# Softmax denominators in six rows of 128 columns, and a 3x3 convolution on two column halves

## What is computed

```
s = jnp.einsum('bhqd,bhkd->bhqk', q, k) / np.float32(np.sqrt(HD))
return jnp.einsum('bhqk,bhkd->bhqd', jax.nn.softmax(s, -1), v)
```

```
x = x + _L1_conv_ref(_gn(x), L1_conv_weight)
t = _to_tokens(x)
```

## Time and profile before

| | |
|---|---|
| median of three runs | 984.92 us (984.06 to 989.01) |
| span of the profiled execution | 980.1 us |
| PE busy | 875.3 us, 89% |
| DVE busy | 595.7 us, 61% |
| ACT busy | 457.1 us, 47% |
| POOL busy | 204.5 us, 21% |
| reciprocals L1676 | 32 of 1756 ns |
| denominators L955 | 1536 instructions, 58.8 us of busy time |
| 3x3 convolution L679 | 80 instructions, 389 ns mean |

### The profile page before, as it was taken

The page is one execution under the profiler, slowest core; times in us unless marked ns, Lnnn a source line. Parts: engine busy times, 40 slices in busy tenths (PEclk is TensorE's granted clock), DMA queues, the critical chain, the costliest instruction groups (busy, mean ns, idle before and its releaser), DMA issues.

```text
span 980.1 us, 22296 instructions
## 1 busy us (share of the span) xinstructions
PE 875.3 (89%) x9216; PEld 588.9 (60%) x9216; DVE 595.7 (61%) x1666; ACT 457.1 (47%) x764; POOL 204.5 (21%) x274
## 2 busy tenths in 40 slices
PE   9888798999999999999999999999988879978876
PEld 8675475566666665666566566656555555644553
DVE  5545534673688468845884588558844764653456
ACT  1003326453555355525543655356435645524754
POOL 1002100120225012401341124112411231131122
PEclk9999689999999999999999999999979999998988
DMA  7100000000000000000000001000100100030000
GB/s 198 25 7 1 1 6 23 23 23 28 23 23 23 28 23 23 23 28 23 23 23 28 7 23 39 23 1 23 39 11 26 36 23 23 23 81 23 2 1 22
DMA packets 25572, 25.84 MB, mean 26 GB/s; under 512 B 14688, under 2 KB 20576, under 8 KB 25344
## 3 DMA queue, kind: packets, MB, share of 16 engines
q1 hardware_dynamic: 25472, 24.42, 8.7%
HBM read 19.69 MB, written 4.72 MB: 25 GB/s over the span
## 4 chain that ended last, share of the span: by engine, by line
PE 58%; DVE 17%; ACT 11%; issue 6%; DMA 5%; POOL 2%; SPq 1%; POOLq 0%; DVEq 0%; ACTq 0%
PE ring L934 7%; PE pv L955 5%; PE side_a L633 5%; PE ring L889 5%; PE pv L973 4%; ACT pr L1190 4%; DVE rden L1676 3%; DMA scale<-branch_scale 3%; PE heads L879 2%; PE side_a L642 2%; PE heads L914 2%; PE ring L929 2%; DMA branch_scale<-rden 2%; PE heads L861 2%; PE ring L897 2%
## 5 line engine op out<-in xcount | busy, mean ns | idle before, releaser
L1190 ACT ACTIVATE pr<-ring 128x1024 f32<-128x1024 f32 (+1 forms) x128 | 120.9, 944 | 108.3 <-PE ring L938 61.0
L934 PE MATMUL ring<-kq 64*128 64x256 f32 (+2 forms) x1280 | 136.5, 341 | 0.7 <-ACT kq L1242 0.5
L934 PEld LDWEIGHTS ring<-kq 64*128 64x128 f32 x1280 | 96.3, 191 | 42.6 <-issue 30.8
L1234 ACT ACTIVATE kq<-ring 128x896 f32<-128x896 f32 x64 | 58.8, 919 | 85.3 <-PE ring L889 85.3
L1686 DVE SCALAR_TENSOR_TENSOR ob<-pv,all_gates,scale 128x256 f32<-128x256 f32 x96 | 46.3, 482 | 85.3 <-PE pv L973 38.4
L1661 DVE TENSOR_REDUCE toks<-heads 128x2 f32<-128x512 f32 x64 | 44.3, 692 | 84.8 <-PE heads L919 83.4
L573 POOL TENSOR_TENSOR toks<-ta,tb 128x128 f32<-128x128 f32 (+1 forms) x96 | 39.7, 434 | 180.4 <-DVE tb L1652 180.4
L1242 ACT ACTIVATE kq<-ring 128x256 f32<-128x256 f32 x64 | 24.6, 384 | 107.5 <-PE ring L897 107.0
L1676 DVE RECIPROCAL rden<-pv 128x256 f32<-128x256 f32 x32 | 56.2, 1756 | 25.5 <-PE pv L955 25.0
L536 POOL TENSOR_TENSOR oT<-ob 128x256 f32<-128x256 f32 x32 | 23.3, 727 | 226.3 <-DVE ob L1686 226.3
L889 PE MATMUL ring<-early,toks 128*128 128x128 f32 x448 | 63.5, 284 | 7.5 <-ACT pr L1190 7.4
(11 more groups left out here) (377 smaller groups left out, 1704.4 us busy)
## 6 DMA issues: line engine op xcount, KB each, us to landing
scale<-branch_scale SPq DMA_DIRECT2D x128, 96.0 KB, 2.3
branch_scale<-rden SPq DMA_DIRECT2D x32, 128.0 KB, 1.7
late<-in_late SPq DMA_DIRECT2D x1, 2158.5 KB, 8.4
xin<-in_x SPq DMA_DIRECT2D x16, 64.0 KB, 2.2
pr<-in_prep SPq DMA_DIRECT2D x1, 602.0 KB, 3.8
y<-ob SPq DMA_DIRECT2D x8, 64.0 KB, 1.9
kq<-in_masks SPq DMA_DIRECT2D x1, 480.0 KB, 8.5
toks<-in_final SPq DMA_DIRECT2D x1, 434.0 KB, 4.4
```

The source lines that it names most:

```text
L934: m = pe.matmul(ring[:, j, at:at + nq], kq[rows, k, key0:key0 + P], kq[rows, k, Q + q_:Q + q_ + nq], start=r % 2 == 0, stop=at > P)
L1190: act.activation(out, in_, ACT.Exp, scale=SCALE).then_inc(S("exp_done"), 1)
L1234: act.activation(kq[:, k, :], flat[:, 0:WIDE], ACT.Copy).then_inc(S("turned"), 1)
```

## The change

`onesk` gets six weights in place of three: for branch br and half x of the queries, a one in column 2 br + x. Row 32j + 2 br + x receives the denominators of 128 queries, so the block is 128x128 in place of 128x256, and so are `rden` and `branch_scale`. The pieces that spanned 256 queries are split; there are eight per head. The four loads spread six rows of 128 numbers over 32 partitions. The rows lie one behind the other in DRAM, so what each load reads and writes is the same 768 numbers as before.

The 3x3 convolution is computed for the upper and the lower 128 pixels on the two halves of PE's columns. The sum with `x1` becomes two instructions, each on 64 partitions, that leave the first 128 pixels on the lower partitions and the second on the upper. One transposition of 128x128 takes the place of two.

```diff
@@ -139,7 +139,7 @@
-        onesk = sb("onesk", [P, BR, 32])
+        onesk = sb("onesk", [P, BR, 2, 32])
@@ -195,9 +195,9 @@
-        rden = sb("rden", [P, T])
+        rden = sb("rden", [P, P])
...
-        scale_out = nc.dram_tensor("branch_scale", (P, T), F32, kind="Internal").ap()
+        scale_out = nc.dram_tensor("branch_scale", (P, P), F32, kind="Internal").ap()
@@ -474,8 +474,9 @@
                     for j in range(4):
-                        sp.dma_start(scale[32 * j:32 * j + 32, :, :], scale_out[32 * j:32 * j + BR, :].unsqueeze(0)
-                                     .broadcast_to((32, BR, T))).then_inc(S("scale_loaded"), 16)
+                        sp.dma_start(scale[32 * j:32 * j + 32, :, :].rearrange("p b (x t) -> p (b x) t", x=2),
+                                     scale_out[32 * j:32 * j + 2 * BR, :].unsqueeze(0).broadcast_to((32, 2 * BR, P)))\
+                            .then_inc(S("scale_loaded"), 16)
 
@@ -676,16 +677,15 @@
                 for i, (copy, dy, dx) in enumerate(PAIRS3):
-                    m = pe.matmul(SA[0:C, 0:T], bin1[:, i, :], window(copy, dy + 1, dx + 1), start=(i == 0),
-                                  stop=(i == 4))
+                    for up in range(2):
+                        m = pe.matmul(SA[C * up:C * up + C, 0:P], bin1[:, i, :], half_window(up, copy, dy + 1, dx + 1),
+                                      start=(i == 0), stop=(i == 4))
                 m.then_inc(S("conv3"), 1)
...
                 pe.sem_inc(S("pe_gap"), 1)
-                for t in range(NT):
-                    m = pe.transpose(SA[:, t * C:(t + 1) * C], x1[0:C, t * P:(t + 1) * P], ident[0:C, 0:C])
-                m.then_inc(S("x2_turned"), 1)
+                pe.transpose(SA[:, 0:P], x1[:, 0:P], ident).then_inc(S("x2_turned"), 1)
                 yield
@@ -948,12 +948,12 @@
                     pe.wait_ge(S("branch_out"), of * 12 + 3 * g)
-                pieces = [(0, 0, T, 0, 0), (0, P, T, 1, 0), (1, 0, T, 0, T),
-                          (2, P, T, 1, P), (2, P, BAND, 1, 3 * P), (2, 0, P, 1, 2 * P)]
-                for i, (br, q_, end, part, a) in enumerate(pieces):
+                pieces = [(0, 0, P, 0, 0), (0, 1, P, 0, P), (0, 1, P, 1, 0), (1, 0, P, 0, T), (1, 1, P, 0, T + P),
+                          (2, 1, P, 1, P), (2, 1, WINDOW, 1, 3 * P), (2, 0, P, 1, 2 * P)]
+                for i, (br, x, n, part, a) in enumerate(pieces):
                     for j in range(4):
-                        m = pe.matmul(PV[32 * j:32 * j + 32, T + q_:T + end], onesk[:, br, :],
-                                      prob(g, j, part, a, end - q_), start=(i == 0), stop=(i == 5))
+                        m = pe.matmul(PV[32 * j:32 * j + 32, T:T + n], onesk[:, br, x, :],
+                                      prob(g, j, part, a, n), start=(i == 0), stop=(i == 7))
                 m.then_inc(S("den_sum"), 1)
@@ -1346,10 +1346,11 @@
                 V.memset(tile[:], 0.0)
-            link(V.memset(onesk[:, :, :], 0.0))
-            V.memset(onesk[:, 0, BR:32], 1.0)
+            link(V.memset(onesk[:, :, :, :], 0.0))
+            V.memset(onesk[:, 0, 0, 2 * BR:32], 1.0)
             for br in range(BR):
-                V.memset(onesk[:, br, br:br + 1], 1.0)
+                for x in range(2):
+                    V.memset(onesk[:, br, x, 2 * br + x:2 * br + x + 1], 1.0)
             link(V.memset(vtok[:, :, P:P + 1], 1.0))
@@ -1455,7 +1456,10 @@
                 after(n, "conv3")
-                V.tensor_tensor(x1[0:C, :], SA[0:C, 0:T], x1[0:C, :], ALU.add).then_inc(S("x2"), 1)
+                for up in range(2):
+                    rows = slice(C * up, C * up + C)
+                    a = V.tensor_tensor(x1[rows, 0:P], SA[rows, 0:P], x1[rows, up * P:up * P + P], ALU.add)
+                a.then_inc(S("x2"), 1)
                 yield
@@ -1673,7 +1677,7 @@
                     dve.wait_ge(S("scale_stored"), of * 64 + 16 * g)
-                V.reciprocal(rden[:, :], PV[:, T:2 * T]).then_inc(S("inverted"), 1)
+                V.reciprocal(rden[:, :], PV[:, T:T + P]).then_inc(S("inverted"), 1)
 
```

## The result

| | before | after |
|---|---|---|
| median of the runs on the same chip | 984.49 us (4 runs, 981.88 to 989.01) | 959.13 us (4 runs, 954.89 to 962.77) |
| span of the profiled execution | 980.1 us | 953.0 us |

The ratio is 0.9742, with a 95% interval from 0.9698 to 0.9785: 25 us less. Lines of after are some lower down in the code: convolutions L634, L643 and L681, sum L1461, transposition L688, reciprocal L1680, first weighting L1690.

The account below looks back on a forecast made before the run. PE, busy 93.92 of 100 us, was taken to bound the kernel, with waits for DVE behind the reciprocal; -12.0 - 4.2 + 0.6 = -15.6 us on 980.1, plus 4.8 from profile to median, gave 969.3 us, range 958 to 979.

Parts of the forecast that it names:

- The reciprocal, -12.0 us: DVE's reciprocal L1676 falls from 256 to 128 columns, 0.80 us less each; 15 on the chain give 12.0 us.
- the 15: Reciprocals, of 32, taken to lie on the chain of waits, from the reciprocal's 2.7% share of it.
- the one on the third groups: At L790 the average wait, 0.96 us, exceeds 0.80; part may be lost on shorter ones, but 12.0 us was kept.
- The store and the loads, 0: Store of 64 KB in place of 128 KB: 0 to 0.85 us each, taken as 0; unchanged loads priced at nothing.
- Rival (b): Behind L790, a shorter wait keeps the clock up: 7.2 us beyond the forecast, 962.1 us; chance 0.15.
- Rival (a): Late-landing loads or another wait hide the gain at L790: only 6.4 us won, 978.5 us; chance 0.19.
- The convolution, -4.2 us: 3x3 convolution on two column halves, 1.26 us for 2.44: 2.2 us in two early images, 2.0 in three second groups.
- The wait at the transposition: Behind the 3x3 convolution PE arrives 1.18 us earlier, DVE only 0.65, so PE waits and 0.65 us is won.
- The 2.2 us of the first two images: There the 3x3 convolution is wholly on the chain: 1.0 us won in the first image, 1.2 in the second.
- The denominators, +0.6 us: Denominators on PE in more, shorter pieces: 1.81 us a group for 1.79, +0.02 us, 32 times.
- rival (d): Shorter denominator sets do not hide their weight loads: 1.54 us a group more, 49 us, 1018 us; chance 0.06.
- Rival (c): PE's halves do not run side by side in the 3x3 convolution: 4.2 us gone, 973.5 us; chance 0.05.

Follow-up runs that it names:

- late_third: Changed kernel with a useless 64 KB transfer, and a wait for it, ahead of the loads in each image's third group: 970.75 us, ratio 0.9845.
- before_first_branch: Kernel before the change with each group's four loads cut in two sets, branch 0 first: 982.71 us, ratio 0.9996.
- den_only: Kernel before plus the denominators' part of the change alone, with the old 3x3 convolution: 960.68 us, ratio 0.9729.
- conv_only: Kernel before plus the 3x3 convolution's part of the change alone, with the old denominators: 984.53 us, ratio 0.9941.
- after_one_load: Changed kernel with the four loads of a group issued as one transfer of 128x768: 1042.2 us, ratio 1.0570.
- recip_twice_third: Changed kernel with a second, unread reciprocal in the third group of each image alone: 965.39 us, ratio 0.9783.
- before_shift: Kernel before with 12 filler products of the start exchanged for 36 of one column, shifting all that follows: 998.63 us, ratio 1.0107.
- after_again: The changed kernel measured once more, without any edit: 959.08 us, ratio 0.9765.
- recip_twice: Changed kernel with a second reciprocal, into a tile nobody reads, in every group: 977.76 us, ratio 0.9893.

## Why the prediction came out as it did

**The reciprocal, -12.0 us: the size of one was right, and half of the count.** Ahead of the 5x5 convolution each image won the 0.80 us to the hundredth. The three second groups with a 3x3 convolution among the 15 won 0.74 as well, but jointly with the convolution; the two of the last images, also among the 15, won nothing (19.70 and 13.93 us before, 20.00 and 14.00 after). The step that failed is the one on the third groups, "single ones are shorter, so part may be lost. I keep 12.0": the mean wait of 0.96 us at L790 was taken for something that every image has. It is a mean over images whose loads land in time, whose passage is 19.85 us before (once 20.18) and after, and images whose loads land late. So the third groups won next to nothing in the regular case, and nearly all of the 11.4 us in the profiles where before had late landings, with what followed from them. In part that is the luck of where they fell, as what stays open below says.

**The store and the loads, 0: mis-sized.** On the page of after the store lands in 1.5 us in place of the 1.7 of the earlier trace rows:

```profile
branch_scale<-rden SPq DMA_DIRECT2D x32, 64.0 KB, 1.5
```

In the third group shown it is 493.88 to 495.43 until the first load can go, 1.55 us, where before had 504.26 to 505.98, 1.72. These 0.17 us with the reciprocal's 0.80 are nearly the room of 0.9 us that late_third measured.

**Rival (b), the clock, priced at 7.2 us with a chance of 0.15, is what the forecast lacked.** In before the two third groups with the longest passages, 22.76 and 27.16 us, are those with a lowered clock behind L790; after they take 19.85. That late_third brings both back and before_first_branch keeps both, the wait and in some images the clock, ties the two together. It does not make the one the measure of the other: in late_third a wait of 0.68 us was followed by the full clock, one of 0.56 us by 0.92. Right would have been a term of its own for late landings, between 0 and 11 us.

**Rival (a) held for the regular third groups alone.** There L790 had a wait of 0 and of 0.27 us in before, so little to win. Where a landing was late, the shorter path did not hide the gain but made it.

**The convolution, -4.2 us: about right in sum, and wrong in its shares.** It takes 1.35 us where 1.26 was worked out. The wait at the transposition came as forecast, 0.51 us. The passage won 0.74 us, for 0.65, in every image, and den_only and conv_only show that neither part wins it alone. The 2.2 us of the first two images can be seen at the first reciprocal: it starts at 159.7 to 161.0 us in seven of the nine profiles of kernels with this part, with a clock of 0.87 to 0.89 from 62 to 141 us, but in the profiles of after and after_one_load at 162.7, as before (162.71). There the clock took the gain back: from 62 to 141 us it was granted 0.81 in both, before 0.85.

**The denominators, +0.6 us: right.** 64 instructions in 1.80 us are 28 ns each. By the Trainium skill, "TensorE: Matmul & The Clock Gate", section "Back-to-back issue gap", 81 ns a matmul of 128 columns, rival (d) would have added 41 us as an estimate; the trace does not agree, with 1.80 us a group in place of 1.79. Rival (c) fell with the 1.35 us.

**The sum.** Of the 10 us between 969.3 and 959.1 the clock and the late landings explain most: 11.4 + 1.9 us in the steady part against the 4 x 0.80 = 3.2 that the sum had for the four third groups among the 15. That the time lies in the range is in part luck, since the sum had no term for them. What the third groups' longer path costs in an average run, and not in the profiled one, was measured only from the other side, and widely: 4 to 6 us by recip_twice_third, and 10 to 12 by the still longer one of late_third.

**What stays open.** Why a load lands late. Over the profiles of before, after, den_only and conv_only, all of the 29 groups whose last load landed over 3.0 us after its issue had a packet of the instruction queue among their loads, and 13 of the other 99 groups. Two third groups of before, the stretch of a late and of a normal one:

```profile
DMA packets 193, 0.41 MB, mean 68 GB/s; under 512 B 64, under 2 KB 64, under 8 KB 192
...
q8 instruction: 1, 0.02, 0.9%
```

```profile
DMA packets 192, 0.39 MB, mean 66 GB/s; under 512 B 64, under 2 KB 64, under 8 KB 192
```

The one packet more is the instructions'. The fetches go with the program: four groups (0, 16, 20 and 22) are late in both profiles of the changed kernel, and the edit of before_shift moved the late ones elsewhere. That the fetches delay the loads was not tried by taking them away. In before four of the nine late landings were in third groups, in after one of five (3.14 us, and its passage stayed at 19.85), in after_again two. So a part of the gain may be this placing, and how much is open. By the sum with 7.07 us, as an estimate, the landings of before on the path of after, 0.97 us shorter, would leave 0.9 of the 3.95 us of waits, and the landings of after on the path of before 1.2 us. Either alone takes most of the waits away, as recip_twice showed for the second, and for the clock behind them there is no such sum.

## What to carry to other kernels

Look whether a wait has the same length in every repetition before multiplying its mean: a mean over a few long ones and many of zero calls for a term of its own, with what follows the long ones, the lowered clock among it. Where two engines meet, as reciprocal and convolution do at the sum, shortening one alone moves the wait to the other; both must be shortened, and the gain is near the smaller of the two (0.74 us of 0.80 and 1.1). A path that ends within some tenths of a us of the other work is worth shortening even where it is off the chain, as room against transfers that land late; what that is worth depends on where they fall.

## What the hardware showed beside

A transfer whose access pattern begins with four heads took 6.9 us to the first use, where four transfers of the same bytes, issued one behind the other in 1.70 us, have landed 2.3 us after the last issue: 25.4% of the DMA engines' share was all it had.

Twelve filler products exchanged for 36 of one column each left PE busy for longer in the first 62 us (55.50 us in place of 52.21), at a granted clock of 0.86 in place of 0.94: part of it at 1.2 GHz in place of 2.4.

Halving a store from 128 to 64 KB took 0.17 us off its landing of 1.70, and cutting a load from 96 to 32 KB 0.4 to 0.5 us off 2.3.
